# Second attention: q and k rows turned once in full, and the score operands stacked by way of DRAM

## What is computed

```python
qkv = jnp.einsum('bld,ed->ble', x, w_qkv)
qkv = qkv.reshape(B, L, 3, H, D).transpose(2, 0, 3, 1, 4)   # H = 16 heads of D = 16
q, k, v = (qkv[0], qkv[1], qkv[2])
q = rmsnorm(q, q_norm_w)
k = rmsnorm(k, k_norm_w)
scores = jnp.einsum('bhqd,bkhd->bhqk', q, k) * scale
attn = jax.nn.softmax(scores, axis=-1)
out = jnp.einsum('bhqk,bhkd->bhqd', attn, v)
```

## Time and profile before

| | us |
|---|---|
| median of 3 runs | 1409.52 (1408.64 to 1409.75) |
| the profiled execution | 1408.91 |
| its span | 1407.1 |
| TensorE busy | 1368.9 (97%) |
| VectorE, ScalarE, GpSimd busy | 920.9, 820.0, 761.9 |
| DMA queue of SyncE | 163.99 MB, 38.3% of 16 engines |

### The profile page before, as it was taken

How to read it: one execution, slowest core, us unless ns; L and a number is a source line. 1 busy time by engine, 2 the same in 40 slices (tenths; PEclk the granted TensorE clock), 3 DMA queues, 4 the chain that set the end, 5 groups by cost and what they waited for, 6 DMA issues and landing times. The chain is left out here.

```text
span 1407.1 us, 25856 instructions
## 1 busy us (share of the span) xinstructions
PE 1368.9 (97%) x8950; PEld 1221.1 (87%) x8950; DVE 920.9 (65%) x1793; ACT 820.0 (58%) x2172; POOL 761.9 (54%) x757
## 2 busy tenths in 40 slices
PE   9999899999999999999999999899999999999997
PEld 7887798999899989998999888788889888889887
DVE  6655566565656565656665665677777878777764
ACT  5553444554544555445544544378787788778873
POOL 2651433454434454435544443477669677777764
PEclk9999999999999999999999999999999999999999
DMA  5995333334332343223433334144233242342442
GB/s 197 323 330 198 85 91 89 92 80 120 100 94 52 101 130 99 75 75 98 114 86 94 113 75 165 68 122 150 83 98 123 68 150 84 120 120 92 143 122 90
DMA packets 85681, 165.64 MB, mean 118 GB/s; under 512 B 16720, under 2 KB 27664, under 8 KB 83248
## 3 DMA queue, kind: packets, MB, share of 16 engines
q1 hardware_dynamic: 85552, 163.99, 38.3%
HBM read 99.90 MB, written 22.09 MB: 87 GB/s over the span
## 5 line engine op out<-in xcount | busy, mean ns | idle before, releaser
L775 POOL TENSOR_TENSOR a_pr<-a_pr,a_ri 128x512 f32<-128x512 f32 x128 | 133.5, 1043 | 299.1 <-DVE a_ri L955 299.1
L832 ACT ACTIVATE a_pr<-a_score,a_nb 128x256 f32<-128x256 f32 x256 | 119.3, 471 | 266.3 <-DVE a_nb L947 266.3
L1337 POOL TENSOR_TENSOR l_pr<-l_pr,l_ri 128x512 f32<-128x512 f32 x128 | 133.5, 1043 | 119.0 <-DVE l_ri L1714 118.1
L1465 ACT ACTIVATE l_pr<-l_score,l_nb 128x256 f32<-128x256 f32 x256 | 119.2, 472 | 80.8 <-DVE l_nb L1680 80.2
L58 PE MATMUL a_job<-s_xs,s_wh 128*128 128x512 f32 x384 | 153.9, 401 | 1.0 <-PEq L221 1.0
L60 PE MATMUL a_job<-s_xs,s_wl 128*128 128x512 f32 x384 | 151.7, 395 | 0.0
L59 PE MATMUL a_job<-s_xs,s_wh 128*128 128x512 f32 x384 | 151.3, 394 | 0.0
L947 DVE TENSOR_REDUCE a_nb<-a_score 128x2 f32<-128x512 f32 x128 | 88.5, 692 | 85.0 <-PE a_score L1026 83.3
L1680 DVE TENSOR_REDUCE l_nb<-l_score 128x2 f32<-128x512 f32 x128 | 87.5, 684 | 34.0 <-PE l_score L1820 33.4
L960 DVE TENSOR_TENSOR a_pt<-a_turn,a_pt 128x512 fp32r<-128x512 f32 x128 | 87.5, 683 | 24.2 <-ACT a_pt L840 24.2
L1844 PE MATMUL l_out<-s_wh,l_vp 128*128 128x256 f32 x512 | 91.6, 300 | 0.9 <-DVE s_wh L1684 0.9
(11 more groups left out here) (257 smaller groups left out, 4780.3 us busy)
## 6 DMA issues: line engine op xcount, KB each, us to landing
s_wl<-wgu_scratch SPq DMA_DIRECT2D x56, 512.0 KB, 4.8
a_sk<-a_rotk SPq DMA_DIRECT2D x384, 64.0 KB, 2.0
a_sq<-a_rotq SPq DMA_DIRECT2D x256, 64.0 KB, 2.0
s_xs<-xn_scratch SPq DMA_DIRECT2D x14, 1024.0 KB, 5.6
l_wd<-wd_scratch SPq DMA_DIRECT2D x56, 256.0 KB, 2.7
a_raw<-in_w SPq DMA_DIRECT2D x30, 256.0 KB, 3.0
wgu_scratch<-f_split SPq DMA_DIRECT2D x14, 512.0 KB, 4.7
f_praw<-in_moe_w SPq DMA_DIRECT2D x14, 384.0 KB, 4.5
```

The costliest lines, as they stand in the source:

```text
L775: pool.tensor_tensor(e, e, ri[:, n % 2, :].unsqueeze(2).broadcast_to([P, 2, SEQ]), ALU.mult)\
L832: i = act.activation(pr[:, n % 2, t, :], PS[n % 2][:, t * SEQ:(t + 1) * SEQ], ACT.Exp, bias=nb[:, n % 2, t:t + 1], accum_out=sm[:, n % 2, ...
L1337: pool.tensor_tensor(e, e, ri[:, n % 3, :].unsqueeze(2).broadcast_to([P, 2, SEQ]), ALU.mult)\
L1465: i = act.activation(pr[:, n % 3, t, :], PS[n % NPS][:, t * SEQ:(t + 1) * SEQ], ACT.Exp, bias=nb[:, n % 3, t:t + 1], accum_out=sm[:, n % 3 ...
```

## The change

`head_columns` reorders the rows of `w_qkv` (and the norm weights) on the host, so that the columns of q and k come as (half, head of a pair, feature, pair): partitions of a turned 128x128 block are then (head of a pair, feature, pair), four pairs to a half. Sums of squares and scaling read in steps of four accordingly. `stq`, `stk`, `k_hi`, `q_hi`, `k_lo`, `q_lo` and the jobs S go. In their place stand two jobs X a batch (`X_AT`: slots 8 and 10, for the first batch 8 and 9): TensorE turns `qk` itself, four transposes a job; ScalarE writes the high parts of q and k to `tqk`, VectorE the low ones. SyncE stores `tqk` to `qs` and `ks` in DRAM, four transfers a half (`store_stack`, in the slot after), and loads from there the stacks of two pairs at a time, three transfers (`load_stack`, every fourth slot, one slot group ahead; the copies come of a source that is read twice). `zq` and `sk` have 4 places. The scores of every fourth head wait for `zq_in` and `sk_in`. `STACK_AT` puts these transfers into SyncE's list, ahead of `load_gu(K)`. `SLOT_GOAL` goes from 30.6 to 28.7, `EARLY_GOAL` from 14 to 18.

```diff
-    NJ, NPS, NSTK, NGU, ND, NCB, NHID = 3, 1, 3, 3, 3, 3, 3
+    NJ, NPS, NSTK, NGU, ND, NCB, NHID = 3, 1, 4, 3, 3, 3, 3
+    PER_LOAD = 2
-    UNIT, SLOT_GOAL, EARLY_GOAL = 10, 30.6, 14
+    UNIT, SLOT_GOAL, EARLY_GOAL = 10, 28.7, 18
+    def X_AT(m):
+        return (8, 9) if m == 0 else (8, 10)
...
-        m, r = divmod(n + 4, H1)
-        if r % 2 == 0 and 0 <= m < BATCH:
-            jobs.append((f"S{r // 2}", m))
+        if b + 1 < BATCH and u in X_AT(b + 1):
+            jobs.append((f"X{X_AT(b + 1).index(u)}", b + 1))
...
+    OPENS = [AT["D1", K - 1 - ND] if K > ND else AT["U", K] - 2 for K in range(L + 1)]
+    STACK_AT = [[n for n in SLOTS if (OPENS[K - 1] if K else SLOTS[0] - 1) < n <= (OPENS[K] if K < L else SLOTS[-1])] for K in range(L + 1)]
...
-        stq, stk = n_.sb("stq", [P, TB, H1, 4, D1]), n_.sb("stk", [P, TB, H1, 4, D1])
-        zq, sk = n_.sb("zq", [P, NSTK, 2, SEQ], F32R), n_.sb("sk", [P, NSTK, SEQ], F32R, shift=OFF)
+        tqk = n_.sb("tqk", [P, 2, 2, 2, SEQ], F32R)
+        zq, sk = n_.sb("zq", [P, 2, NSTK, SEQ], F32R), n_.sb("sk", [P, NSTK, SEQ], F32R, shift=OFF)
...
+                def store_stack(m, half):
+                    wait_free(sp, (f"X{half}", m))
+                    for low in range(2):
+                        sp.dma_start(qs_dram[m % 2, half, :, :, low].rearrange("h d p n -> (h d) p n"), tqk[:, half, 0, low, :].bitcast(F32))                           .then_inc(tqk_out[half], 16)
+                        sp.dma_start(ks_dram[m % 2, half, :, low].rearrange("h d p n -> h (d p) n"), tqk[:, half, 1, low, :].bitcast(F32))                           .then_inc(tqk_out[half], 16)
+                def load_stack(i):
+                    pair = i * PER_LOAD
+                    m, p = divmod(pair, H1 // 2)
+                    at = slice(pair % NSTK, pair % NSTK + PER_LOAD)
+                    if p % 4 == 0:
+                        sp.wait_ge(tqk_out[p // 4], 16 * 4 * (m + 1))
+                    if pair >= NSTK:
+                        sp.wait_ge(S["score_full"], 2 * (pair + PER_LOAD - NSTK))
+                    half, j = divmod(p, 4)
+                    for h in range(2):
+                        own = qs_dram[m % 2, half, h, :, :, j:j + PER_LOAD].rearrange("d c p n -> (d c) (p n)")
+                        sp.dma_start(zq[64 * h:64 * h + 64, h, at, :].bitcast(F32).rearrange("r p n -> r (p n)"),
+                                      own.unsqueeze(0).broadcast_to([2, 2 * D1, PER_LOAD * SEQ])).then_inc(zq_in[stack_of(i)], 16)
+                    own = ks_dram[m % 2, half, :, :, :, j:j + PER_LOAD].rearrange("h c d p n -> (h c d) (p n)")
+                    sp.dma_start(sk[:, at, :].bitcast(F32).rearrange("r p n -> r (p n)"),
+                                  own.unsqueeze(1).broadcast_to([4 * D1, 2, PER_LOAD * SEQ])).then_inc(sk_in[stack_of(i)], 16)
+                def transfers(n):
+                    m, u = n // H1 + 1, n % H1
+                    if m < BATCH and u - 1 in X_AT(m):
+                        store_stack(m, X_AT(m).index(u - 1))
+                    if n % (2 * PER_LOAD) == 0 and 0 <= n // (2 * PER_LOAD) + 1 < N // (2 * PER_LOAD):
+                        load_stack(n // (2 * PER_LOAD) + 1)
...
+                    for n in STACK_AT[K]:
+                        transfers(n)
...
-                    elif name[0] == "S":
-                        pair = m * (H1 // 2) + int(name[1])
-                        r = pair % NSTK
+                    elif name[0] == "X":
+                        half = int(name[1])
-                        if pair >= NSTK:
-                            act.wait_ge(S["score_full"], 2 * (pair - NSTK) + 2)
-                        for h in range(2):
-                            act.activation(zq[64 * h:64 * h + 64, r, h, :], bank[64 * h:64 * h + 64, 0:SEQ], ACT.Copy)
-                        act.activation(sk[:, r, :], bank[:, SEQ:2 * SEQ], ACT.Copy).then_inc(free_of(item), 1)
+                        if m >= 1:
+                            act.wait_ge(tqk_out[half], 16 * 4 * m)
+                        act.activation(tqk[:, half, :, 0, :], bank[:, :].rearrange("p (r n) -> p r n", r=2), ACT.Copy).then_inc(S["turned_hi"], 1)
...
-                            dve.wait_ge(S["q_lo"], 4 * m)
-                            dve.wait_ge(S["k_lo"], 4 * m)
+                            wait_full(dve, ("X1", m - 1))
+                    elif name[0] == "X":
+                        half = int(name[1])
+                        dve.wait_ge(S["turned_hi"], 2 * m + half + 1)
+                        dve.tensor_tensor(tqk[:, half, :, 1, :], bank[:, :].rearrange("p (r n) -> p r n", r=2),
+                                          tqk[:, half, :, 0, :], ALU.subtract).then_inc(free_of(item), 1)
...
-                    own(dve.tensor_reduce(ss[:, :], sqr[:, :, :].rearrange("p t (g d) -> p (t g) d", d=D1), AX.X, ALU.add))
+                    own(dve.tensor_reduce(ss[:, :].rearrange("p (g q) -> p g q", q=4), sqr[:, :, :].rearrange("p t (g d q) -> p (t g) q d", d=D1, q=4), AX.X, ALU.add))
...
-                    elif name[0] == "S":
-                        p = int(name[1])
-                        pe.wait_ge(S["q_lo"], 4 * m + 2 * (p // 4) + 2)
-                        pe.wait_ge(S["k_lo"], 4 * m + 2 * (p // 4) + 2)
-                        for k, rows in enumerate((stq, stk)):
+                    elif name[0] == "X":
+                        half = int(name[1])
+                        pe.wait_ge(S["weighted"], m + 1)
+                        for part in range(2):
-                                i = pe.transpose(bank[:, k * SEQ + t * P:k * SEQ + (t + 1) * P],
-                                                 rows[:, t, 2 * p:2 * p + 2, :, :].rearrange("p h r d -> p (h r d)"), ident[:, :])
+                                at = part * D + half * P
+                                i = pe.transpose(bank[:, part * SEQ + t * P:part * SEQ + (t + 1) * P], qk[:, t, at:at + P], ident[:, :])
...
-                    if u % 2 == 0:
-                        wait_free(pe, (f"S{u // 2}", m))
+                    if u % (2 * PER_LOAD) == 0:
+                        i = n // (2 * PER_LOAD)
+                        pe.wait_ge(zq_in[stack_of(i)], 16 * 2 * (n // (2 * NSTK) + 1))
+                        pe.wait_ge(sk_in[stack_of(i)], 16 * (n // (2 * NSTK) + 1))
-                        i = pe.matmul(PS[n % NPS][:, t * SEQ:(t + 1) * SEQ], zq[:, r, u % 2, t * P:(t + 1) * P], sk[:, r, :],
+                        i = pe.matmul(PS[n % NPS][:, t * SEQ:(t + 1) * SEQ], zq[:, u % 2, r, t * P:(t + 1) * P], sk[:, r, :],
...
+    qs = nc.dram_tensor("qs_scratch", [2, 2, 2, D1, 2, 4, SEQ], F32, kind="Internal").ap()
+    ks = nc.dram_tensor("ks_scratch", [2, 2, 2, 2, D1, 4, SEQ], F32, kind="Internal").ap()
...
+def head_columns(w):
+    import numpy as np
+    qk = w[0:2 * D].reshape(2, 2, 4, 2, D1, D).transpose(0, 1, 3, 4, 2, 5).reshape(2 * D, D)
+    return np.concatenate([qk, w[2 * D:]])
```

More of the change, by code:

```diff
@@ L1077, in _, with stage_layer1 @@
                 rest(PS[(N - 2) % 2], 9)
-def stage_layer1(nc, sh, l1, wgu_dram, wd_dram, ct_dram, out):
+def stage_layer1(nc, sh, l1, wgu_dram, wd_dram, ct_dram, qs_dram, ks_dram, out):
     N = BATCH * H1
     L = MT * NSTEP
-    NJ, NPS, NSTK, NGU, ND, NCB, NHID = 3, 1, 3, 3, 3, 3, 3
+    NJ, NPS, NSTK, NGU, ND, NCB, NHID = 3, 1, 4, 3, 3, 3, 3
+    PER_LOAD = 2
     SLOTS = range(-H1, N + 5)
@@ L1196, in stage_layer1 @@
         gu_in = l1.gu_in
+        zq_in, sk_in = ([n_.sem(f"{s}_in{i}") for i in range(NSTK // PER_LOAD)] for s in ("zq", "sk"))
+        tqk_out = [n_.sem(f"tqk_out{i}") for i in range(2)]
         d_in, cb_in = ([n_.sem(f"{s}_in{i}") for i in range(3)] for s in ("d", "cb"))
@@ L1212, in wait_full, with stack_of @@
             engine.wait_ge(S["job_full"], JOB[item] + 1)
+        def stack_of(i):
+            return i % (NSTK // PER_LOAD)
         def bank_of(item):
@@ L1223, in tokens @@
             return slice(at, at + P)
-        def heads(t, part, half):
-            at = part * D + half * P
-            return qk[:, t, at:at + P].rearrange("p (h d) -> p h d", d=D1).unsqueeze(2).broadcast_to([P, 8, 2, D1])
-        def half_of(rows, t, half):
-            return rows[:, t, 8 * half:8 * half + 8]
         def wait_merged(engine, s):
@@ L1313, in weigh @@
                         .then_inc(S["weighted"], 1)
-                def q_lo(m, half, t):
-                    pool.wait_ge(S["q_hi"], 4 * m + 2 * half + t + 1)
-                    pool.tensor_tensor(half_of(stq, t, half)[:, :, 1::2, :].bitcast(F32R), heads(t, 0, half),
-                                       half_of(stq, t, half)[:, :, 0::2, :], ALU.subtract).then_inc(S["q_lo"], 1)
                 def spread(m, a):
@@ L1442, in job_out @@
                             act.activation(gt[:, m % 2, :], bank[:, :], ACT.Tanh, scale=0.5).then_inc(S["tanh_ready"], 1)
-                def k_hi(m, half):
-                    act.wait_ge(S["scaled"], m + 1)
-                    if m >= 1:
```

(28 more changed lines are left out.)

15 lines of the change are left out of this document (3 added, 12 removed).

## The result

The changed kernel takes 1501.82 us (median of 4 runs, 1500.59 to 1503.94) against 1409.41 for the kernel before in the same session (1408.64 to 1409.75): ratio 1.0658, 95% interval [1.064, 1.0677]. That is 92 us slower, where +59 was forecast. The profiled execution took 1502.34 us, its span 1500.5.

What follows compares the result with a forecast made beforehand. TensorE, 97% busy, was taken to set the pace before the change, two full DMA engines to delay loads after it. -16.8 + 3 - 8 + 60 + 13 + 8 = +59 gave 1469 us, range 1400 to 1505.

Steps and rivals of the forecast that it cites:

- the two engines: zq loads and k stores run on 2 of 16 DMA engines, busy 54.8 of 55.8 us a batch.
- Signs: Expected if right: no landing times, gate/up tiles later than 4.8 us, DMA share near 0.5, first score near 936.
- Always the same two: Assumption, shown by no row, that zq loads and k stores always fall on the same two DMA engines.
- the bunch: Transfers queue up from slot 8, the next stack comes late for slot 15: 8.5 us x 7 batches, +60 (+35 to +108).
- the clock: TensorE's clock drops after stops: 1 us for each of 8 stops, +8 (0 to +16).
- the walk: SyncE's queue followed from slot 8 in issue order: stack landed about 34 us, needed at 24.5 by slot 15.
- The start: Stores, tiles and first stack ahead of the second attention's first score: 936.5 instead of 923.4, +13 us (+9 to +22).
- further relief: Less work on ScalarE, VectorE, GpSimd: -2 if slots stay tight, -8 if TensorE has other pauses.
- The sum so far is ... 1393 us, if every load is on time: Last stage without late transfers: TensorE's saving -16.8, relief -2, X's wait +3, about -16 us.
- Rival 3: Loads on time, another engine as bound; gain lost in waits of the turn and X: 1402 to 1412, chance 0.05.
- X's wait, +3: X in slot 8 waits for GpSimd's weighting of q: 0.5 us x 7 batches, +3 (0 to +10).
- Planner's goals, no saving in the sum: New goals move 24 matmuls, 5.6 us, ahead of the first score; early stretch longer, slots shorter, no saving.

Runs made afterwards that it cites:

- e4: Changed kernel with zq loads split into plain 32-row loads and rows reordered so that each k store is one piece of 128 rows; 1422.2 us.
- e6: e4 with gate/up tiles 3 and 4 and down tile 2 requested ahead of the stores, first stack ahead of the combine rows' store; 1419.5 us.
- e7: e4 with ScalarE writing the squares in head order, so that VectorE's sum reads 16 neighbours; 1417.9 us.
- e11: e4 with e6's order, e7's squares, and X in slots 9 and 11 of every batch but the first; 1410.8 us.
- e9: e4 with GpSimd's normalising of the second 128 queries of each head left out (result incomplete); 1413.4 us.
- e10: Kernel before, with GpSimd's normalising of the second 128 queries of each head left out (result incomplete); 1404.1 us.
- e5: Changed kernel with each zq load split in two by columns, first size still 2; 1504.2 us.
- e3: Changed kernel with each zq load split into two plain 32-row loads and each k store into two of 64 rows; 1429.5 us.
- e8: e4 with the planner's goals of before (slot goal 30.6, early goal 14); 1445.9 us.

## Why the prediction came out as it did

The direction, its cause and the range (1400 to 1505) held; the size was 33 us short. The time lies 3 us below the upper edge: the range was wide because the transfers' price was uncertain, and what used it up was mostly another term, as the following shows. The ledger, in us, from the traces and from the prediction's own terms (last column: from the last score to the end of the span):

| | first score | 127 slots | behind |
|---|---|---|---|
| before | 918.7 | 465.1 | 23.3 |
| forecast, loads on time | 923.4 | 444 | 23.3 |
| e4 (narrow transfers gone) | 936.3 | 462.9 | 21.9 |
| forecast | 936 | 506 | 23.3 |
| changed kernel | 945.7 | 532.9 | 21.9 |

**Right: the two engines.** Signs, price and rate came as put down: no landing times, gate/up tiles far above 4.8 us, a mean share below 0.5, 24.5 KB/us where 23 was taken. "Always the same two", which was assumed, is borne out by the zq loads that end one behind the other. Of the signs only the first score near 936 failed (945.7). The narrow transfers cost 76 us in the forecast (1393 to 1469) and 79.6 by e4, or somewhat more if e4's additional transfers cost time.

**Right in sum, wrong in its parts: the bunch and the clock.** Forecast were 8.5 us a batch and 1 us of clock. From first score to first score of the last batch the changed kernel needs (1425.9 - 945.7) / 7 = 68.6 us a batch, e4 (1349.1 - 936.3) / 7 = 59.0: 9.6 against 9.5. But the walk ended at a stack late for slot 15. The trace shows gate/up tiles first, 35.4 us of waiting in the slots against 15.8 for scores; they stop slot 11 of every second batch (2.3 to 4.1 us) and mostly slots 12 and 14 of the others (0.9 to 12.5). The walk had the tile "late for a part of it" and priced it with the stack. The start lost 9.4 us to the two engines, not 13.

The split between the bunch and the clock was wrong, and that their sum came out is luck. In the 127 slots e4 has 2928 matmuls and is busy with them 430.5 us; the changed kernel has 2926 and is busy 455.9 us. It has the half clock (1.2 GHz) for 68.0 us of these slots, in twelve stretches that each begin in or right behind a wait for a tile or a stack; e4 has it for 6.8 us. So of the 70.0 us between the two, up to 25.4 are the lower clock (an upper bound, since a faster TensorE would have waited more for the same tile), where +8 (0 to +16) was put down; 44.6 are time without a matmul, where +60 less 6 of further relief was put down.

**The step that failed: "The sum so far is ... 1393 us, if every load is on time".** e4 and the time it gives, 1422, stand 29 us over it; that is nearly all of the 33. TensorE's saving is real: in the six middle batches it is busy 327.4 us in e4 against 343.4 before, 16.0 less, 12.6 of it transposes by the forecast's price and the rest matmuls moved ahead of the first score. But those batches take 354.4 us against 354.8: 27.0 us without a matmul instead of 11.4. The forecast took TensorE's 97% for a bound that would follow its work down, and relief of the other engines as a further gain of 2 to 8. Rival 3 described what happens (gain lost in waits of the turn and of X, up to 1412) and got 0.05; e4 is 10 us over even its edge. By the ledger e4 is 12.9 us over the forecast at the first score and 18.9 in the slots, and 1.4 under behind them; the profiled execution was 0.8 us slower than the median. Of these:
- The start, 12.9: "TensorE would be at its first score at 923.4". It left out that SyncE waits for X0's bank with the gate/up tiles' requests behind it, although the walk of the queue had them in that order. e6 takes 4.2 us off the first score, 2.7 off the end. About 1.5 us are none of this: the down tile that both kernels ask for near 890, ahead of any X, is asked for at 891.4 in e4's trace and at 889.9 before. The rest of the start was not taken apart.
- The slots, 18.9. The strided sum of squares, which the forecast priced at nothing beside TensorE's work, is worth 4.3 (e7). The Trainium skill, "Advanced Engine Details and Errata", section "Memory Cachelines", speaks of a penalty when each access opens another line; the trace agrees, 1208 to 2012 ns. It was named and put at zero as work beside TensorE's; but VectorE works in a fixed order, and its length shows in the next slot. X one slot later gives up to 4.4 (e11 less e6 and e7), with slot 108 as the place. The normalising accounts for 3.7 more than before (e9, e10), with the doubt named there. The eight additional transfers of e4 are unpriced between 2.4 (e5's eight more a batch, on the narrow kernel) and 15 (an estimate: twice the step from e4 to e3). These overlap, and no exact split was made: which of them holds most of the 18.9 us stays open.

**X's wait, +3**: 2.3 us in the changed kernel, 3.6 in e4. **Planner's goals, no saving in the sum**: e8 shows that they are worth 23.7 us in e4. The claim that moved work is neither gain nor loss was wrong there; how they weigh with the narrow transfers was not run.

## What to carry to other kernels

Read the first size of both sides of every transfer in the built program: one with 2 used two engines here, its bytes can be small beside the rest, and yet it delays the last two shares of the wide transfers queued behind it, wherever those are waited for. Split by rows, not by columns, and look for the damage at the other loads. Price the clock from the number and length of TensorE's stops: here they cost up to a third of what the late loads cost. And 97% busy says little of what comes next: work taken off such an engine comes back as gain only where the slots' other chains and the queue that feeds them are shorter than the new slot; count them before crediting it, with every wait that one sequencer has ahead of unrelated requests.
